# Reordering the work ahead of a mixture-of-experts loop: smaller one-hots, split gathers, a shorter index chain

## The chip, the cores and the metric

The kernel runs on one core of a Trainium2 chip. The engines of the core are TensorE (PE), VectorE (DVE), ScalarE (ACT), GpSimd (POOL) and SyncE (SP, here only an issuer of DMAs). The metric is the device time of one execution in microseconds, as the median of several runs.

## The reference

Four batches of 512 rows of width 256 go through two residual layers. Cut to what matters:

```python
# layer 1, per batch: x normed twice, through W_in, plus "depool" of the context
h = rmsnorm(layernorm(x), g_res) @ W_in + b_in
c = rmsnorm(ctx)[:, :256] * g_init
s[t] = a * s[t-1] + k * c[t]                       # a, k constants
plug = clip(cumsum(boundary_mask) - 1, 0, 1600)    # boundary_mask[cumsum(patch_lens) - 1] = 1
x = x + s[plug] + h
# layer 2: mixture of 8 experts, the best two of each row
p = softmax(layernorm(x) @ gate_w); w, e = top_k(p, 2); w = w / sum(w)
x = x + sum over the two of  w * (silu(z @ w1[e]) * (z @ w3[e])) @ w2[e]
```

The patch lengths (1601 per batch, integers) are an input, so the plug of a row is known only when their running sum has been taken: a mask has a one at each running sum less one that lies below 512, and the running sum of that mask says which row of the scan is added.

## The kernel before

Each engine has a program of its own, written out by hand in the order in which it issues; engines wait for one another on semaphores, and nothing else sets the order. The loop over about 37 blocks of 128 gathered rows (the experts' matmuls, all from the helper at L1545, and the elementwise work around them) begins at about 102 us and lasts to the end. It is not touched. What is touched is the work ahead of it, which goes through the four batches b = 0 to 3, each of TPB = 4 tiles of 128 rows.

The steps, by the names that they have in the code. **lengths** (VectorE): bytes of the lengths are scanned (L795), PE adds up the partitions (`prefix`, L1371), and a chain of short operations of 52 elements, each waiting for the one before, gives for each of the 13 x 4 columns the position below 512. **position(b)**: thirteen comparisons with 0..127 (L853) make a one-hot of the low seven bits, `onehot_lo`; `onehot_hi` is one of the two high bits (L843). **boundaries(b)** (PE, L1378): 13 matmuls of one against the other count the positions, 128 x 4 to a batch. **plugs** (VectorE L860, PE L1387 to L1391, VectorE L865, L868): mask, its running sum by a triangle of ones, `plugi` as indices for the gathers.

**stats_first(b)** (L875 to L886): mean and variance of x, and the sum of squares of the context that ScalarE's **squares(b)** (L616) made. **pow1(b)** (GpSimd, L490): the roots. **norm_first(b)**: on VectorE the scaled context `hp` (written L902, tile name hmul), on ScalarE the normed x (L625). **depool(b)** (PE, L1410, L1412): the scan as matmuls with a decay matrix. **depooled(b)** (VectorE, L910), **dep_out(b)** (SP): its rows to memory. **turned(b)** (PE, L1398): transposes of the normed x; **transposed_first(b)** (ScalarE, L634) copies them to memory. **through_win(b)** (PE, L1432): them through W_in, sixteen passes. **gather(b)** (GpSimd, L500): four indirect DMAs fetch rows of the depool by `plugi`. **second(b)** (VectorE, L919, L925, L928): x plus gathered rows plus through_win, and the statistics of the sum. **pow2(b)** (GpSimd, L506), **norm_second(b)** and **z(b)** (ScalarE, L643): the second norm. **router(b)** (PE, L1398 on z), copies (ScalarE, L651), **logits_of(b)** (PE, L1452), **route(b)** (VectorE): the choice of experts and each row's place in its expert's list.

At the end **lists** (PE, L1481) makes the list of row numbers per block, and VectorE turns it into indices: second_choice L1179, number L1182, unused L1185, idx_all L1188, gidx L1191, by which GpSimd gathers the rows of the first blocks (L529). blocks_i and five `stepm` operations (L1193 to L1203), steps (L1206) and some thirty more short ones make a table of control words, which all engines read before the loop (`table`, L1253). **keep_clock** (PE, L1488) is a matmul of zeros, 128 x 512, whose result nobody reads.

The buffers that tie the steps together: `ctx_sb` holds two contexts, so loads of contexts 2 and 3 wait for batches 0 and 1 (`next_ctx` on SP); `dg` holds gathered rows of two batches; `hp`, `nb1`, `vin` and the turned x have one or two.

## Time and profile before

| what | us |
|---|---|
| median of 3 runs | 444.62 (444.39 to 445.95) |
| the profiled execution | 445.63 |
| its span | 443.8 |
| PE busy in the span | 405.7 (91%) |
| VectorE busy | 303.2 (68%) |
| GpSimd busy | 243.2 (55%) |
| ScalarE busy | 193.7 (44%) |

The span is what the profiler saw of the core; the time of an execution has some 1.8 us around it. Busy shares are means over a loop and a prologue with different limits. In the rows below a line starts with its time in the span, then its duration, the engine, the source line and operation, what it writes and reads, and how many instructions it stands for; in brackets stands how long the engine idled before it and what ended that.

### The profile page before, as it was taken

To read this page: it belongs to the slowest core of one execution; us is meant where nothing else is said; L and a number is where in the kernel's file an instruction comes from. 1 tells how busy PE (TensorE), PEld (TensorE's weight loads), DVE (VectorE), ACT (ScalarE), POOL (GpSimd) and SP (SyncE) were. 2 spreads that over 40 slices of the span, in tenths; PEclk is the share of its full clock that TensorE was granted. 3 is DMA by queue.
4 is the path that set the end of the run, shared out by engine and by line. 5 is a ranking of instruction groups with operands and counts; after the bars stand their busy time and mean duration, and the time that the engine had idled before them with its cause. 6 is when DMAs were issued, how large, how long until landed. Compare 5 with 4: busy or idle time off the path is not lost.

```text
span 443.8 us, 12041 instructions
## 1 busy us (share of the span) xinstructions
PE 405.7 (91%) x2300; PEld 338.6 (76%) x2305; DVE 303.2 (68%) x826; ACT 193.7 (44%) x335; POOL 243.2 (55%) x251
## 2 busy tenths in 40 slices
PE   0669899969899999999999999999999999999983
PEld 0557686536678888888888888888888888788873
DVE  7995959887775577647775775577587546857450
ACT  2573527104543454335544553455445335634341
POOL 6328444313664676546665685576577445435443
PEclk9997969698999999999999999999999999999998
DMA  6953996702895788567887787789788655465652
GB/s 188 356 172 100 303 358 206 289 26 58 265 278 177 198 259 246 178 168 194 243 264 209 228 250 205 194 247 251 202 265 254 197 159 152 127 154 130 166 144 36
DMA packets 80362, 89.82 MB, mean 202 GB/s; under 512 B 8071, under 2 KB 60583, under 8 KB 80343
## 3 DMA queue, kind: packets, MB, share of 16 engines
q1 hardware_dynamic: 64327, 55.24, 38.4%
q0 software_dynamic: 16016, 34.37, 30.7%
q8 instruction: 6, 0.10, 0.1%
q14 instruction: 13, 0.11, 0.1%
HBM read 58.77 MB, written 30.82 MB: 202 GB/s over the span
## 4 chain that ended last, share of the span: by engine, by line
PE 70%; issue 3%; DVE 3%; ACT 1%; DMA 1%; DVEq 1%; POOL 0%; ACTq 0%; POOLq 0%
PE bank L1545 67%; PE bank L1552 2%; ACT split L341 1%; DMA out<-yblk,itok 1%; PE bank L1488 1%; DVE onehot_lo L1173 0%; POOL out L546 0%; ACT yblk L718 0%; DVE hT L1288 0%; DVE hmul L1272 0%; DVEq L295 0%; DVE swap_in L1280 0%; ACTq L341 0%; PE bank L1481 0%; DVE ctx_sb L951 0%
## 5 line engine op out<-in xcount | busy, mean ns | idle before, releaser
L1545 PE MATMUL bank<-split,xT_hi 128*128 x592 | 166.1, 402 | 4.4 <-issue 2.7
L1545 PEld LDWEIGHTS bank<-split,xT_hi 128*128 128x128 f32 x592 | 106.5, 189 | 27.9 <-issue 8.6
L1545 PEld LDWEIGHTS bank<-split,hT 128*128 128x128 f32 x888 | 111.5, 189 | 5.5 <-issue 1.5
L1545 PE MATMUL bank<-split,hT 128*128 (+1 forms) x888 | 113.3, 284 | 1.4 <-ACT yblk L718 0.7
L711 ACT ACTIVATE gact<-bank 128x512 f32<-128x512 f32 x74 | 44.3, 598 | 138.5 <-PE bank L1545 136.2
L1272 DVE TENSOR_TENSOR hmul<-gact,bank 128x512 f32<-128x512 f32 x74 | 50.8, 686 | 74.4 <-ACT gact L711 73.8
L1545 PE MATMUL bank<-split,xT_lo 128*128 x296 | 92.2, 393 | 0.0
L529 POOL DMA_INDIRECT xblk<-z_rows,gidx x40 | 41.0, 1024 | 89.6 <-DVE gidx L1295 69.8
L546 POOL DMA_INDIRECT out<-yblk,itok x37 | 71.0, 1919 | 32.1 <-issue 29.6
L347 DVE TENSOR_TENSOR split<-raw,split x22 | 50.3, 2292 | 25.9 <-ACT split L341 24.2
L1545 PEld LDWEIGHTS bank<-split,xT_lo 128*128 128x128 f32 x296 | 55.6, 188 | 12.3
L1280 DVE STREAM_TRANSPOSE swap_in<-hmul 128x512 f32<-128x512 f32 x74 | 52.6, 711 | 4.4
L1288 DVE TENSOR_TENSOR hT<-swap_out,hT 128x512 fp32r<-128x512 f32 x74 | 50.5, 683 | 4.8 <-ACT hT L706 3.8
L537 POOL DMA_INDIRECT wtok<-w_rows,widx x37 | 46.5, 1257 | 13.0 <-issue 11.0
L341 ACT ACTIVATE split<-raw (+1 forms) x24 | 45.8, 1915 | 7.5 <-issue 6.1
L280 POOL DMA_DIRECT2D raw<-in_L_ffn_w x56 | 38.0, 684 | 18.5 <-issue 18.5
L706 ACT ACTIVATE hT<-swap_out 128x512 fp32r<-128x512 f32 x74 | 46.5, 628 | 2.9 <-issue 2.0
L718 ACT ACTIVATE yblk<-bank,wtok 128x256 f32<-128x256 f32 x37 | 17.2, 464 | 34.9 <-PE bank L1545 32.3
L283 POOL DMA_DIRECT2D raw<-in_L_ffn_w x28 | 20.1, 724 | 5.3 <-issue 4.9
L1432 PE MATMUL bank<-win,batch 128*128 128x256 f32 x64 | 20.7, 495 | 0.8 <-DVE win L1101 0.5
L1488 PE MATMUL bank<-zeros,ones_b 128*128 128x512 bf16 x69 | 19.5, 435 | 1.5 <-issue 1.4
L1432 PEld LDWEIGHTS bank<-win,batch 128*128 128x128 f32 x64 | 16.0, 257 | 4.4 <-DVE x_all L925 0.7
(199 smaller groups left out, 336.0 us busy)
## 6 DMA issues: line engine op xcount, KB each, us to landing
raw<-in_L_ffn_w POOLq DMA_DIRECT2D x84, 256.0 KB
swap_rows<-swap_in SPq DMA_DIRECT2D x74, 256.0 KB, 3.7
swap_out<-swap_rows SPq DMA_DIRECT2D x74, 256.0 KB, 3.7
ctx_sb<-in_ctx SPq DMA_DIRECT2D x4, 1024.0 KB, 6.4
raw<-in_L_ffn_w SPq DMA_DIRECT2D x12, 256.0 KB, 6.6
x_all<-in_x SPq DMA_DIRECT2D x4, 512.0 KB, 8.4
depool_rows<-gact SPq DMA_DIRECT2D x4, 512.0 KB, 4.0
out<-x_all SPq DMA_DIRECT2D x4, 512.0 KB, 6.2
```

The costliest lines, as they stand in the source:

```text
L280: eng.dma_start(raw_up[:, ds(slot, 1), m, n >> 1, cols], rows).then_inc(signal, 16)
L341: act.activation(split_chunk[:, ds(raw3 * 2 + m, 1)], raw_chunk[:, ds(raw3 + m, 1)], ACT.Copy)\
L347: dve.tensor_tensor(split_chunk[:, ds(raw3 * 2 + m + 3, 1)], raw_chunk[:, ds(raw3 + m, 1)], split_chunk[:, ds(raw3 * 2 + m, 1)].bitcast(f3 ...
L529: pool.indirect_dma_start(xblk[:, q, :], None, z_dram[:, :], bass.IndirectOffsetOnAxis(ap=gidx[:, q:q + 1], axis=0))\
L537: pool.indirect_dma_start(wtok[:, q:q + 1], None, w_dram[:, :], bass.IndirectOffsetOnAxis(ap=widx[:, q:q + 1], axis=0))\
L546: pool.indirect_dma_start(out[:, :], bass.IndirectOffsetOnAxis(ap=itok[:, q:q + 1], axis=0), yblk[:, q, :], None, compute_op=ALU.add).then ...
L706: act.activation(hT_hi[:, q, ks].rearrange("p k (a t) -> p a k t", a=NQ), swap_out[:, q, part], ACT.Copy)\
L711: act.activation(gact[:, half * HALF:(half + 1) * HALF], p_gate[half][:, :], ACT.Silu)\
L1272: dve.tensor_tensor(hmul[:, cols], gact[:, cols], p_lin[part][:, :], ALU.mult)\
L1280: dve.transpose(swap_in[:, q, part].rearrange("p b k t -> p k b t"), hmul[:, part * HALF:(part + 1) * HALF].rearrange("p (k b t) -> p k b ...
L1288: dve.tensor_tensor(hT_lo[:, q, ks].rearrange("p k (a t) -> p a k t", a=NQ), swap_out[:, q, part], hT_hi[:, q, ks].bitcast(f32).rearrange( ...
L1545: mm = pe.matmul(out_, xp, w_, start=start and n == 0, stop=stop and n == 2)
```

## The change

- The positions are split as 32 by 16 in place of 128 by 4 (`LO`, `HI`). The one-hots of all batches are made by two comparisons over broadcast operands (`position_low`, `position_high`), and the 52 matmuls follow one another, 32 x 16 each. The mask is then 32 rows by (batch, tile, quarter), and the running sum takes 16 small matmuls with a triangle `upto_b`, which GpSimd makes and ScalarE copies.
- On VectorE the sums of x of batch 0 stand between the scan and the carries of the lengths (they wait for x of batch 0), its squares amid the last of the length operations; plugs and the mask move forward; the addition of through_win (`through_added`) moves from behind the gathered rows to ahead of them, and `second` adds the gathered rows last.
- Contexts 2 and 3 get memory of their own (the raw weights' second buffer, loaded later), all contexts and x are loaded in one sequence without waits; ScalarE squares two contexts in a row. The first raw load of that buffer waits for the last use of the contexts.
- Gathers are issued two tiles at a time, between the pow operations on GpSimd; two gathers of batches 2 and 3 each now stand ahead of pow2(0) and pow2(1).
- PE: 18 keep_clock matmuls behind the prefix and 5 behind the transposes of W_in; plugs ahead of depool(1); turned(1), turned(2), turned(3) each later by one depool or through_win; the first block's transposes ahead of the wait for the table. ScalarE's order of the copies and norms from norm_first(2) on is as before.
- Lists: rows of z are stored from row 1 on, row 0 is zeros, so the number in the list is the index. gidx comes straight from the list; unused and idx_all are made behind the table (`row_places`), and blocks_i and the stepm operations stand ahead of the wait for the lists. The GpSimd semaphore step ahead of the first two block gathers is left out.

The diff, cut to its core (renamed buffers, and bodies that only have other constants, are left out):

```diff
+            upto = zT[0:LO, 0:NA // 2, :].rearrange("p j d -> p (j d)").rearrange("p (a t) -> p a t", a=NA)
+            upto_b = zT[0:LO, NA // 2, :].bitcast(bf16).rearrange("p (a t) -> p a t", a=NA)
...
+            pos_lo = onehots[:, 0:B * CH * LO].rearrange("p (n c) -> p n c", c=LO)
+            pos_hi = onehots[:, B * CH * LO:B * CH * (LO + HI)].rearrange("p (n c) -> p n c", c=HI)
...
+        def ctx_of(b):
+
+            if b < 2:
+                return ctx_sb[:, b]
+            return raw[:, 1, (b - 2) * TPB * CD:(b - 1) * TPB * CD].rearrange("p (j d) -> p j d", d=CD)
...
-                sp.dma_start(ctx_sb[:, b % 2], ctx[b, 0:S, :].rearrange("(j p) d -> p j d", p=P))\
+                sp.dma_start(ctx_of(b), ctx[b, 0:S, :].rearrange("(j p) d -> p j d", p=P))\
...
-            load_x(1)
-            load_ctx(1)
-            load_x(2)
-            load_x(3)
+            for b in range(1, B):
+                load_ctx(b)
+                load_x(b)
...
-            next_ctx(2)
             dep_out(0)
-            next_ctx(3)
             dep_out(1)
...
+            pool.memset(upto, 1.0).then_inc(s["upto_ready"], 1)
+            pool.wait_ge(s["upto_ready"], 1)
+            pool.affine_select(out=upto, in_=upto, compare_op=ALU.is_ge, fill=0.0,
+                               base=0, pattern=[[-LO, NA], [1, P]], channel_multiplier=-1)\
+                .then_inc(s["upto_ready"], 1)
...
             pow1(1)
+            gather(0, (0, 1))
             pow1(2)
-            gather(0)
+            gather(0, (2, 3))
             pow1(3)
             gather(1)
+            gather(2, (0, 1))
             pow2(0)
-            gather(2)
+            gather(2, (2, 3))
+            gather(3, (0, 1))
             pow2(1)
-            gather(3)
+            gather(3, (2, 3))
             pow2(2)
             pow2(3)
...
             squares(0)
+            act.wait_ge(s["upto_ready"], 2)
+            act.activation(upto_b, upto, ACT.Copy).then_inc(s["upto_ready"], 1)
             norm_first(0)
             squares(1)
+            squares(2)
             transposed_first(0)
-            squares(2)
             norm_first(1)
+            squares(3)
             transposed_first(1)
-            squares(3)
             norm_first(2)
...
+            def position_low():
+
+                full3 = [P, NBC, LO]
                 dve.wait_ge(s["iota_ready"], 3)
-                dve.tensor_tensor(onehot_hi[:, :, :], iota_m8[:, :].unsqueeze(1).broadcast_to([P, NBC, TPB]),
-                                  hif.unsqueeze(2).broadcast_to([P, NBC, TPB]), ALU.is_equal)\
-                   .then_inc(s["onehot_ready"], 1)
-
-            def position(b):
-
-                if b >= 2:
-                    dve.wait_ge(s["count_ready"], b - 1)
-                for k in range(CH):
-                    n = b * CH + k
-                    ins = dve.tensor_scalar(onehot_lo[:, b % 2, k, :], iota_b[:, :], low[:, n:n + 1], None,
-                                            ALU.is_equal)
-                ins.then_inc(s["onehot_ready"], 1)
+                dve.tensor_tensor(pos_lo, iota_f[:, 0:LO].unsqueeze(1).broadcast_to(full3),
+                                  low.unsqueeze(2).broadcast_to(full3), ALU.is_equal).then_inc(s["onehot_ready"], 1)
+
+            def position_high():
+
+                full3 = [P, NBC, HI]
+                dve.wait_ge(s["carry_step"], lengths_done[0])
+                dve.tensor_tensor(pos_hi, iota_less[:, :].unsqueeze(1).broadcast_to(full3),
+                                  hif.unsqueeze(2).broadcast_to(full3), ALU.is_equal).then_inc(s["onehot_ready"], 1)
...
+            def through_added(b):
+
+                dve.wait_ge(s["hn_ready"], TPB * (b + 1))
+                xb = x_all[:, b * TPB:(b + 1) * TPB, :]
+                for n in range(PAIRS):
+                    dve.wait_ge(s["hmm_ready"], b * TPB + 2 * n + 2)
+                    dve.tensor_tensor(pair(xb, n), pair(xb, n), pH[n][:, :], ALU.add).then_inc(s["xh_ready"], 1)
...
-            lengths()
-            stats_first(0)
-            position(0)
+            lengths_scanned()
+            sums_first(0)
+            lengths_placed(lengths_carried(), lambda: squares_in(0))
             norm_first(0)
-            position(1)
+            position_low()
+            position_high()
+            depooled(0)
+            plugs()
             stats_first(1)
-            position(2)
-            depooled(0)
+            plugs_end()
+            scale_win()
             norm_first(1)
-            position(3)
             stats_first(2)
             depooled(1)
-            plugs()
-            scale_win()
-            plugs_end()
             norm_first(2)
             stats_first(3)
+            through_added(0)
             depooled(2)
             norm_first(3)
             second(0)
             depooled(3)
+            through_added(1)
             norm_second(0)
             second(1)
             norm_second(1)
             route(0)
+            through_added(2)
             second(2)
             places_beside_route(0)
             norm_second(2)
+            through_added(3)
...
-            dve.wait_ge(s["list_mm"], 1)
-            dve.tensor_copy(second_choice[:, :], p_idx)\
-               .then_inc(s["idx_step"], 1)
-            dve.wait_ge(s["idx_step"], 1)
-            dve.scalar_tensor_tensor(number[:, :], p_idx, -1.0, second_choice[:, :], ALU.mult, ALU.max)\
-               .then_inc(s["idx_step"], 1)
-            dve.wait_ge(s["idx_step"], 2)
-            dve.scalar_tensor_tensor(unused[:, :], number[:, :], 0.0, ids_f[:, B * TPB:B * TPB + 1]
-                                     .broadcast_to([P, TABLE]), ALU.is_equal, ALU.mult).then_inc(s["idx_step"], 1)
-            dve.wait_ge(s["idx_step"], 3)
-            dve.scalar_tensor_tensor(idx_all[:, :], number[:, :], -1.0, unused[:, :], ALU.add, ALU.add)\
-               .then_inc(s["idx_ready"], 1)
-            dve.wait_ge(s["idx_ready"], 1)
-            dve.tensor_copy(gidx[:, :], idx_all[:, 0:2]).then_inc(s["gidx_ready"], 2)
...
+            dve.wait_ge(s["list_mm"], 1)
+            dve.tensor_copy(second_choice[:, :], p_idx)\
+               .then_inc(s["idx_step"], 1)
...
+            dve.scalar_tensor_tensor(gidx[:, :], p_idx[:, 0:2], -1.0, second_choice[:, 0:2], ALU.mult, ALU.max)\
...
-            def boundaries(b):
-
-                pe.wait_ge(s["onehot_ready"], b + 2)
-                for k in range(CH):
-                    mm = pe.matmul(p_count[:, b * TPB:(b + 1) * TPB], onehot_lo[:, b % 2, k, :],
-                                   onehot_hi[:, b * CH + k, :], start=(k == 0), stop=(k == CH - 1))
+            def boundaries():
+
+                pe.wait_ge(s["onehot_ready"], 2)
+                for b in range(B):
+                    for k in range(CH):
+                        n = b * CH + k
+                        mm = pe.matmul(p_count[:, b * HI:(b + 1) * HI], pos_lo[:, n, :], pos_hi[:, n, :],
+                                       start=(k == 0), stop=(k == CH - 1))
                 mm.then_inc(s["count_ready"], 1)
...
+                for a in range(NA):
+                    pe.matmul(p_plug, upto_b[:, a, :], bmask[:, :, :, a].rearrange("p b j -> p (b j)"),
+                              start=(a == 0), stop=False)
...
             prefix()
+            pe.wait_ge(s["pad_ready"], 1)
+            pe.wait_ge(s["bf16_ready"], 2)
+            keep_clock(18)
 
             pe.wait_ge(s["small_in"], 16 * 5)
             for k in range(KD):
@@ -1495,24 +1545,22 @@
                     mm = pe.transpose(p_win[:, k * D + m * P:k * D + (m + 1) * P], win[:, m, k * P:(k + 1) * P],
                                       ident[:, :])
             mm.then_inc(s["wT_ready"], 1)
-            boundaries(0)
+            keep_clock(5)
             depool(0)
+            boundaries()
             turned(0)
-            boundaries(1)
-            boundaries(2)
+            plugs()
             depool(1)
-            boundaries(3)
-            turned(1)
-            plugs()
             through_win(0)
             depool(2)
-            turned(2)
+            turned(1)
             depool(3)
             through_win(1)
+            turned(2)
             router(0)
-            turned(3)
             logits_of(0)
             through_win(2)
+            turned(3)
             router(1)
...
+            xT(0, 0, 0)
             pe.wait_ge(s["table_ready"], 1)
             less_two = blocks_less_two(pe)
-            xT(0, 0, 0)
             keep_clock(4)
```

Three places in the order. First VectorE at the one-hots: in the kernel before (onehot_lo is written by position, hmul is the scaled context, gact the depooled rows, st and vin the statistics of x)

```order
L853 TENSOR_SCALAR onehot_lo<-iota_b,ln_v 128x128 x13
L894 SCALAR_TENSOR_TENSOR nb<-mv,rs 128x4
L902 SCALAR_TENSOR_TENSOR hmul<-ctx_sb,rs,ginit 128x256 x4
L853 TENSOR_SCALAR onehot_lo<-iota_b,ln_v 128x128 x13
L875 BN_STATS st<-x_all 128x6 x4
L878 BN_AGGR mv<-st 128x2 x4
L882 TENSOR_SCALAR vin<-sumsq 128x4
L886 TENSOR_SCALAR vin<-mv 128x4
L853 TENSOR_SCALAR onehot_lo<-iota_b,ln_v 128x128 x13
L910 TENSOR_TENSOR gact<-bank,bin 128x512 x2
```

and in the changed kernel, from the scaled context of batch 0 on:

```order
L936 SCALAR_TENSOR_TENSOR hmul<-ctx_sb,rs,ginit 128x256 x4
L873 TENSOR_TENSOR onehots<-iota_f,ln_v 128x1664
L880 TENSOR_TENSOR onehots<-iota_less,ln_v 128x832
L944 TENSOR_TENSOR gact<-bank,bin 128x512 x2
L886 TENSOR_SCALAR bmask<-bank 32x64
L901 BN_STATS st<-x_all 128x6 x4
L904 BN_AGGR mv<-st 128x2 x4
```

The four groups of thirteen comparisons, between which the steps of batches 0 and 1 stood, are two operations in a row, and the statistics of batch 1 now stand behind the mask, which waits for the counts.

Second PE around through_win(1) and (2) (win), with turned (bank from batch), router (from z) and logits (gate). Before:

```order
L1432 MATMUL bank<-win,batch 128x256 x8
L1398 MATMUL bank<-ident,z 128x128 x8
L1398 MATMUL bank<-ident,batch 128x128 x8
L1452 MATMUL bank<-gate,batch 128x8 x8
L1432 MATMUL bank<-win,batch 128x256 x8
L1398 MATMUL bank<-ident,z 128x128 x8
```

In the changed kernel:

```order
L1484 MATMUL bank<-win,batch 128x256 x8
L1450 MATMUL bank<-ident,batch 128x128 x8
L1450 MATMUL bank<-ident,z 128x128 x8
L1504 MATMUL bank<-gate,batch 128x8 x8
L1484 MATMUL bank<-win,batch 128x256 x8
L1450 MATMUL bank<-ident,batch 128x128 x8
L1450 MATMUL bank<-ident,z 128x128 x8
```

turned(3) stood between the first router and its logits; now turned(2) stands ahead of that router and turned(3) behind through_win(2).

Third VectorE behind the lists matmul (bank). Before:

```order
L1179 COPY second_choice<-bank 128x43
L1182 SCALAR_TENSOR_TENSOR number<-bank,second_choice 128x43
L1185 SCALAR_TENSOR_TENSOR unused<-number,ids_f 128x43
L1188 SCALAR_TENSOR_TENSOR idx_all<-number,unused 128x43
L1191 COPY gidx<-idx_all 128x2
L1193 TENSOR_SCALAR blocks_i<-cum 1x1
L1197 TENSOR_SCALAR stepm<-cum,ids_f 128x8
L1198 TENSOR_SCALAR stepm<-cum,ids_f 128x8
L1199 SCALAR_TENSOR_TENSOR stepm<-cum,ids_f,nblk 128x8
L1201 TENSOR_SCALAR stepm<-cum,ids_f 128x8
L1203 TENSOR_SCALAR stepm<-cum,ids_f 128x8
L1206 TENSOR_REDUCE steps<-stepm 128x5
```

In the changed kernel, where the wait for the lists is ahead of second_choice:

```order
L1218 TENSOR_SCALAR blocks_i<-cum 1x1
L1222 TENSOR_SCALAR stepm<-cum,ids_f 128x8
L1223 TENSOR_SCALAR stepm<-cum,ids_f 128x8
L1224 SCALAR_TENSOR_TENSOR stepm<-cum,ids_f,nblk 128x8
L1226 TENSOR_SCALAR stepm<-cum,ids_f 128x8
L1228 TENSOR_SCALAR stepm<-cum,ids_f 128x8
L1232 COPY second_choice<-bank 128x43
L1235 SCALAR_TENSOR_TENSOR gidx<-bank,second_choice 128x2
L1237 SCALAR_TENSOR_TENSOR number<-bank,second_choice 128x43
L1241 TENSOR_REDUCE steps<-stepm 128x5
```

The six operations that need no list now come ahead of it, and two of the five that need it are gone from here.

## Rows read from the trace of the kernel before

**Rows 1.** the page, chain of work that ended last, shares of the span by line

```profile
PE bank L1545 67%; PE bank L1552 2%; ACT split L341 1%; DMA out<-yblk,itok 1%; PE bank L1488 1%; DVE onehot_lo L1173 0%; POOL out L546 0%; ACT yblk L718 0%; DVE hT L1288 0%; DVE hmul L1272 0%; DVEq L295 0%; DVE swap_in L1280 0%; ACTq L341 0%; PE bank L1481 0%; DVE ctx_sb L951 0%
```

**Rows 2.** chain of waits of 90 to 104 us: start us, us, what

```profile
93.65 0.21 DVE number L1182
...
95.53 0.21 DVE stepm L1203
...
100.25 0.68 PE bank L1552 x2
100.94 1.71 PE bank L1488 x4
102.64 1.38 PE bank L1545 x4
```

**Rows 3.** groups by line, VectorE, 0-104 us: xcount, busy us, mean ns, idle before

```profile
L853 DVE TENSOR_SCALAR onehot_lo<-iota_b,ln_v 128x128 bf16<-128x128 bf16 x52 | 8.8, 241 | 0.0
...
L1173 DVE TENSOR_TENSOR onehot_lo<-iota_f,blk 128x688 f16<-128x688 f32 x2 | 1.7, 868 | 0.0
```

**Rows 4.** timeline of PE: start us, us, engine line op out<-in xcount [idle before]

```profile
12.75 1.11 PE L1495 MATMUL bank<-ident,win 128*128 128x128 f32 x4 [6.83 <-DMA gate<-in_L_ffn_gate_w]
...
16.20 2.04 PE L1410 MATMUL bank<-hmul,decayT 128*128 128x256 f32 x4
...
25.21 1.10 PE L1410 MATMUL bank<-hmul,decayT 128*128 128x256 f32 x4 [1.27 <-DVE hmul L902]
...
28.42 0.48 PE L1378 MATMUL bank<-onehot_hi,onehot_lo 128*128 128x4 bf16 x13
28.76 1.07 PE L1398 MATMUL bank<-ident,batch 128*128 128x128 f32 x8
...
32.41 6.75 PE L1432 MATMUL bank<-win,batch 128*128 128x256 f32 x16 [0.50 <-DVE win L1101]
39.00 1.03 PE L1410 MATMUL bank<-hmul,decayT 128*128 128x256 f32 x4
...
47.07 3.72 PE L1432 MATMUL bank<-win,batch 128*128 128x256 f32 x16 [0.29 <-DVE x_all L925]
...
56.71 6.54 PE L1432 MATMUL bank<-win,batch 128*128 128x256 f32 x16
...
64.52 1.92 PE L1452 MATMUL bank<-gate,batch 128*128 128x8 f32 x16 [0.22 <-ACT batch L651]
...
78.45 2.56 PE L1452 MATMUL bank<-gate,batch 128*128 128x8 f32 x16
```

**Rows 5.** windows, PE: stretch, us, busy us, granted clock, DMA share, GB/s

```profile
33.00:35.00 2.00, 2.00 (x6) 0.50 0.61 194
```

**Rows 6.** timeline of ScalarE

```profile
12.10 0.19 ACT L616 ACTIVATION_READ_ACCUMULATOR xblk<-ctx_sb 128x1 f32 x1
...
42.72 1.08 ACT L634 ACTIVATE batch<-bank 128x512 f32<-128x512 f32 x2 [6.72 <-PE bank L1398]
43.69 2.07 ACT L625 ACTIVATE batch<-x_all,nb,rs 128x256 f32<-128x256 f32 x4
50.31 2.08 ACT L643 ACTIVATE z<-x_all,nb,rs 128x256 f32<-128x256 f32 x4 [4.55 <-DVE nb L939]
...
68.97 2.08 ACT L643 ACTIVATE z<-x_all,nb,rs 128x256 f32<-128x256 f32 x4 [4.10 <-DVE nb L939]
```

**Rows 7.** timeline of GpSimd

```profile
30.37 1.64 POOL L490 TENSOR_TENSOR rs<-vin,neg_half 128x8 f32<-128x8 f32 x1 [7.33 <-DVE vin L886]
...
34.41 0.97 POOL L500 DMA_INDIRECT dg<-depool_rows,plugi  x1 [0.30 <-issue]
```

**Rows 8.** timeline of VectorE

```profile
24.59 1.66 DVE L902 SCALAR_TENSOR_TENSOR hmul<-ctx_sb,rs,ginit 128x256 f32<-128x256 f32 x4
...
28.29 1.39 DVE L875 BATCH_NORM_STATS2 st<-x_all 128x6 f32<-128x256 f32 x4
...
61.88 1.23 DVE L919 TENSOR_TENSOR x_all<-x_all,dg 128x1024 f32<-128x1024 f32 x1 [2.61 <-DMA dg<-depool_rows,plugi]
```

134 lines of the change are left out of this document (75 added, 59 removed).

## Prediction, made before the changed kernel had run

> **What bounds the kernel now.** First the page's shares of the chain: two thirds of the span are the expert matmuls of the loop [rows 1]. The diff leaves the loop's work alone, so the change is worth what it moves the loop's first matmul, which starts at 102.64 in the chain of waits [rows 2]. Then the stretch ahead of it, engine by engine. The lists are copied out in the two operations that end at 93.86 (the second is L1182) and the chain from there is VectorE [rows 2]. What the lists wait for is z of batch 2, which ScalarE begins at 68.97 after VectorE's routing of batch 1; that follows logits(1) on PE, 64.52 + 1.92 = 66.44, by 2.53 us [rows 4, 6]. From z(2) on the order is the same in both kernels, so the question is when logits(1) ends. Before that point no engine is full: PE waits 1.27 for VectorE ahead of depool(1), ScalarE 6.72 for PE, VectorE 2.61 for gathered rows [rows 4, 6, 8]. The third thing to see is PE's clock. through_win(0) and (2) take 6.75 and 6.54 us, through_win(1) 3.72 for the same sixteen passes, and the granted clock inside the first of them is 0.50, the lower of its two levels, 1.2 GHz against 2.4 [rows 4, 5].
>
> The profiled run took 445.63 us with a span of 443.8; the median of the three runs is 444.62. I sum differences of the profiled execution and take them off the median.
>
> **One-hots: much work saved, little time.** 52 comparisons, 8.8 us of VectorE, go [rows 3]. Two wide ones come, 1664 and 832 elements per partition. Nearest rows: 688 elements in 0.868 and 1024 in 1.23 [rows 3, 8], so 1.08 ns for each further element: 1.23 + 640 x 1.08 ns = 1.92, and 0.868 + 144 x 1.08 ns = 1.02, 2.94 together (3.15 if all went at 0.868/688; 2.6 at the slope alone). VectorE is spared some 6 us. But the order decides. squares(0) ends at 12.29 [rows 6]; with about 0.3 for two small operations, 1.64 of pow [rows 7] and 1.66 of scaling [rows 8], VectorE reaches the one-hots at 15.9 and ends them at 18.8. The 52 count matmuls, at 0.48 for 13 [rows 4], end at 20.7; the mask takes 0.2; then stats_first(1), which from its start to its pow took 30.37 - 28.29 = 2.08 [rows 7, 8], then pow 1.64: 24.6. With 0.15 and a first product of 0.45, depool(1) starts at 25.2. Before it started at 25.21 [rows 4]. The one-hots used to fill the time in which pow and the counts were awaited; now VectorE waits instead. This part: 0.
>
> **23 keep_clock matmuls.** They lie where PE idled 6.83 for the last small load [rows 4]. From 5.92 on, 18 of them take 7.7 at the half-clock rate of 1.71 for four [rows 2], then the transposes 1.1, then five more 2.2: 16.9 at the latest; depool(0) can have its first input at 14.9. Before, its first four matmuls took 2.04, against 1.10 for those of depool(1) [rows 4]. If the full clock comes in the 18, depool(0) needs 3.2 and is done before the counts can start at 18.8: cost 0. If it never comes, depool(0) needs about 5.9 and ends at 22.8: 4.0 late. I take 0, since a long dense run brought the clock back in through_win(0), whose next matmuls are fast again [rows 4]. The Trainium skill ("TensorE: Matmul & The Clock Gate", What's actually happening) says that the idle state is the throttled one and activity releases it; that agrees with the slow first matmuls, and by it too the cost here is 0.
>
> **PE from depool(1) on.** A depool at full clock is 28.42 - 25.21 = 3.2 [rows 4]. A through_win is 3.55 net: in through_win(0) the next matmul starts 0.16 before the row ends [rows 4]. After a turned, ScalarE starts 0.55 later (half of 1.07) and ends its copies 0.97 after that; norm_first takes 2.07, z 2.08 [rows 4, 6].
> plugs is now ahead of depool(1), so through_win(0) follows directly: 25.2 + 3.2 + 3.55 = 31.95 (before 39.0, with a half-clock pass). depool(2) to 35.15. turned(1) comes behind it, and its copies and norm_first(2) end at 35.15 + 0.55 + 0.97 + 2.07 = 38.75. Scaling of batch 3 (0.6 to the first product) and depool(3): 42.55. through_win(1): 46.1, before 50.8. Here turned(2) now stands, and ScalarE still has its copies and norm_first(3) ahead of z(0): 46.1 + 3.59 = 49.7, z(0) to 51.8, before 52.4 (50.31 + 2.08) [rows 6]. PE's lead of 4.7 us shrinks to 0.6: this is the new wait that the order brings. A copy of 0.55 and logits(0), 1.92: 54.3. through_win(2) to 57.8, before 63.25. turned(3), 0.55 and 0.97, and z(1), 2.08: 61.4. The copy and logits(1): 63.9, before 66.44. Gain at z(2): 2.5 us, if no pass falls to half clock.
>
> **Gathers and own context memory.** Each gather costs GpSimd 0.97 + 0.30 [rows 7]. Two of batch 2 now stand ahead of pow of z(0): 2.5 us later there. z(0) cannot start before 49.7 for ScalarE's sake, which covers it; without that cover it costs up to 2.5. The early gathers remove VectorE's wait of 2.61 [rows 8], but logits(1) is next late, so no gain beyond the 2.5 above. Contexts 2 and 3 in the raw buffer drop a wait on SP; at most 0.
>
> **Lists to loop.** From 93.86 to 95.74 VectorE runs unused, idx_all, gidx, blocks_i and five stepm operations [rows 2]: 1.88. The first two leave the chain, the last six move into the wait for the lists, which is about 0.6 long for 0.9 of work (0.3 stays), and a narrow gidx (0.2) stays: gain 1.4. PE's transposes of block 0, 0.68 [rows 2], move ahead of the table; VectorE's xT_lo is next late about half a microsecond earlier than 102.64: gain 0.5 (0 to 0.7).
> Behind z(2) logits(3) took 2.56 against 1.92 [rows 4], a half-clock stretch too; without it another 0.6.
>
> **Sum at full clock:** 2.5 + 1.4 + 0.5 + 0.6 = 5.0, so 439.6.
>
> **The clock, and the rivals.** In the sum PE idles or runs only transposes and narrow matmuls in three places ahead of dense passes: 20.7 to 25.2, 35.2 to 39.4, and 46.1 to 54.3. Before, such stretches ended differently: the one that ends at 25.21 left depool(1) at full rate, those of 28.42 to 32.41 and 50.8 to 56.71 were followed by half-clock passes [rows 4, 5]. A fall costs 6.75 - 3.72 = 3.0 or 6.54 - 3.72 = 2.8, less what it loses in slack: 2.3 to 3.0, taken as 2.7. The third stretch, longer than either that brought the fall before, is the likeliest place.
>
> *Forecast, one fall:* 5.0 - 2.7 = 2.3 gained, 442.3. Chance 0.33.
> *No fall (rival 1):* 439.6; for it speak the 23 extra matmuls and plugs in the first stretch. 0.27, and 0.05 for still more, about 437, should the early loads and gathers pull VectorE forward where I found it waiting.
> *Two falls (rival 2):* 5.0 - 5.4 = 0.4 slower, 445.0. The gain of the index chain is given back. 0.17.
> *Three falls (rival 3, the other side):* 5.0 - 8.1 = 3.1 slower, 447.7. It decides when all of through_win(0), (1) and (2) read 6.5 us or more, against two of three before. The Trainium skill's table ("Why this matters for your kernels", same page) speaks against idle gaps between matmul bursts in the middle of a kernel, and by it all three gaps would count; the trace bears that out in two of three cases. 0.10.
> *The warm-up does not do what it says (rival 4):* depool(0) at half rate, 4.0 of delay against 5.0 of gain, 443.6, or 446.3 with a fall. 0.08.
>
> **How the numbers follow.** The predicted time is the forecast's, 442.3. The range must leave out 2 in 10: from 438.0, below rival 1, to 447.5, where rival 3 begins. Half a per cent, 2.2 us, is about what a measurement of this kernel can tell from no change. Faster by more than that: no fall and better, 0.32, and about half of the forecast's case, 0.16: 0.48. Within: the rest of it, most of rival 2 and some of rival 4: 0.34. Slower: 0.18.
>
> **What would show it.** After the change: onehots in two rows of 1.9 and 1.0; VectorE idle for the counts and the pow around 20 to 25; depool(1) at about 25; the three through_win rows near 3.7, one perhaps 6 or more; ScalarE idle for PE ahead of the copies of turned(1), (2) and (3); z(2) near 66 to 69; VectorE's two operations between list and steps. The forecast is wrong if depool(1) starts well before 25 (then the one-hots do pay), if z(0) waits for GpSimd, or if the loop itself, with its first raw loads and gathers moved, changes its length of 341 us.

## The result, and the profile after

The changed kernel takes 456.12 us (median of 4 executions, 452.55 to 457.01); the kernel before, on the same chip, 444.5 (4 executions, 442.07 to 445.95). The ratio is 1.025, with a 95% interval of 1.018 to 1.032: slower by 11.6 us, outside the forecast range of 438.0 to 447.5.

The profiled execution took 457.01 (span 455.4) against 445.63 (span 443.8). Its 11.6 us of span split at three marks:

| stretch | before | after | difference |
|---|---|---|---|
| start to the end of the lists matmul (L1481, now L1533) | 93.37 | 103.13 | +9.76 |
| lists to the loop's first matmul | 8.96 | 7.11 | -1.85 |
| from there to the loop's first silu (gact on ScalarE) | 3.56 | 3.11 | -0.45 |
| first silu to the end | 337.91 | 342.05 | +4.14 |

The gain of the index chain is there, but not made up as forecast. VectorE's rows behind the lists, before and after:

```profile
99.15 0.19 DVE L1253 CAST table<-bank 1x43 int32<-1x43 f32 x1 [0.33 <-PE bank L1537]
99.46 2.29 DVE L1312 TENSOR_TENSOR split<-raw,split 128x2048 fp32r<-128x2048 f32 x1
101.67 0.42 DVE L1265 TENSOR_TENSOR xT_lo<-bank,xT_hi 128x256 fp32r<-128x256 f32 x1
```

```profile
107.07 0.19 DVE L1288 CAST table<-bank 1x43 int32<-1x43 f32 x1 [0.33 <-issue]
107.37 2.29 DVE L1355 TENSOR_TENSOR split<-raw,split 128x2048 fp32r<-128x2048 f32 x1
109.58 0.42 DVE L1308 TENSOR_TENSOR xT_lo<-bank,xT_hi 128x256 fp32r<-128x256 f32 x1
```

The table starts 5.78 behind the lists before and 3.94 after, so 1.84 is won by then. From the table to xT_lo it takes 2.52 before and 2.51 after, since VectorE is busy with split: PE's earlier transposes of the first block bring nothing. The 0.45 ahead of the first silu is the clock: on the loop's first matmuls PE's windows of one microsecond show a granted clock of 0.50 at 102 to 103 and 0.79 at 103 to 104 in the kernel before, and 1.00 at 110 to 114 after; the first four take 1.69 and 1.20.

Two losses outweigh the gain, one in the prologue and one in the loop, of which the diff changes one copy and the operations in front of it.

For the prologue, first PE by stretches of ten microseconds (stretch, its length in us, busy us and instructions, granted clock, DMA share, GB/s):

```profile
20.00:30.00 10.00, 6.83 (x47) 0.68 0.61 214
30.00:40.00 10.00, 8.22 (x41) 0.98 0.36 119
40.00:50.00 10.00, 8.30 (x26) 0.66 0.92 279
50.00:60.00 10.00, 6.67 (x35) 0.71 0.88 285
60.00:70.00 10.00, 8.52 (x36) 0.78 0.51 160
70.00:80.00 10.00, 9.95 (x50) 0.66 0.41 139
```

A stretch of ten with a granted clock of c had 20 x (1 - c) us at the lower level, 1.2 GHz. Added up, that is 30.7 us of the sixty (from the same windows at one microsecond each); the kernel before has 14.1, nearly all in the two slow passes of [rows 4]. The timeline of PE tells where (start us, us, engine line operation, what it writes and reads, count, idle before and what ended it):

```profile
18.80 1.47 PE L1428 MATMUL bank<-onehots 128*32 128x16 bf16 x52 [0.57 <-DVE onehots L880]
...
24.95 2.04 PE L1462 MATMUL bank<-hmul,decayT 128*128 128x256 f32 x4 [3.17 <-DVE hmul L936]
...
30.71 3.62 PE L1484 MATMUL bank<-win,batch 128*128 128x256 f32 x16
...
41.70 2.04 PE L1462 MATMUL bank<-hmul,decayT 128*128 128x256 f32 x4 [3.48 <-DVE hmul L936]
...
55.44 2.07 PE L1450 MATMUL bank<-ident,z 128*128 128x128 f32 x8 [3.33 <-issue]
57.31 3.58 PE L1504 MATMUL bank<-gate,batch 128*128 128x8 f32 x16
60.74 5.54 PE L1484 MATMUL bank<-win,batch 128*128 128x256 f32 x16
66.12 1.04 PE L1450 MATMUL bank<-ident,batch 128*128 128x128 f32 x8
68.53 1.81 PE L1450 MATMUL bank<-ident,z 128*128 128x128 f32 x8 [1.38 <-ACT z L659]
...
70.57 2.89 PE L1504 MATMUL bank<-gate,batch 128*128 128x8 f32 x16
73.31 6.08 PE L1484 MATMUL bank<-win,batch 128*128 128x256 f32 x16
...
87.84 3.06 PE L1504 MATMUL bank<-gate,batch 128*128 128x8 f32 x16
```

Five pieces of dense work run at the lower level: depool(1) at 24.95 (four matmuls in 2.04, against 1.10 in [rows 4]), depool(3) at 41.70, logits(0) with through_win(2), the end of logits(1) with through_win(3), and logits(3). Ahead of the first three PE idled 3.2 to 3.5 us, ahead of the others it had transposes and narrow matmuls with short waits. The first follows a wait for VectorE's scaled context, which ahead of the same depool(1) took 1.27 in [rows 4] and left the clock up.

The lateness reaches ScalarE through the copies of the turned x, which in its order stand ahead of the next norm (timeline of ScalarE; L650 are these copies, L659 is z):

```profile
51.77 1.08 ACT L650 ACTIVATE batch<-bank 128x512 f32<-128x512 f32 x2 [10.91 <-PE bank L1450]
...
66.81 1.08 ACT L650 ACTIVATE batch<-bank 128x512 f32<-128x512 f32 x2 [8.67 <-PE bank L1450]
...
75.98 2.07 ACT L659 ACTIVATE z<-x_all,nb,rs 128x256 f32<-128x256 f32 x4 [5.00 <-DVE nb L976]
```

z(1), behind the second of these rows, starts at 67.79, and z(2) at 75.98, against 68.97 in [rows 6].

The loop's loss shows in the page's groups (count, busy us, mean ns) and at its start on VectorE:

```profile
L1593 PE MATMUL bank<-split,xT_hi 128*128 x592 | 167.8, 405 | 4.8 <-issue 2.3
...
L1593 PE MATMUL bank<-split,xT_lo 128*128 x296 | 93.0, 395 | 0.0
```

```profile
112.17 0.20 DVE L1293 SCALAR_TENSOR_TENSOR unused<-number,ids_f 128x43 f32<-128x43 f32 x1
...
113.12 0.20 DVE L1303 TENSOR_TENSOR widx_all<-unused,second_choice 128x43 int32<-128x43 f32 x1
115.38 0.69 DVE L1315 TENSOR_TENSOR hmul<-gact,bank 128x512 f32<-128x512 f32 x1 [2.06 <-issue]
```

The first silu had ended at 113.95, and hmul follows 1.43 later: the five row_places operations, and what VectorE's sequencer issues behind them without a busy row, come in between. In the kernel before three such operations stand there, and they end at 104.77, 1.72 ahead of the end of the silu.

### The profile page after: what moved, and what is told of

Its sections match the earlier page's. It is cut to its first block and busy times, and to the rows that moved or that the text cites. A ratio compares the mean times of both kernels' runs of the same rounds, so it can differ in the third digit from the quotient of the medians.

```text
span 455.4 us, 12058 instructions
## 1 busy us (share of the span) xinstructions
PE 417.6 (92%) x2334; PEld 344.1 (76%) x2339; DVE 297.9 (65%) x775; ACT 194.1 (43%) x336; POOL 243.9 (54%) x253
## 5 line engine op out<-in xcount | busy, mean ns | idle before, releaser
L1593 PE MATMUL bank<-split,xT_hi 128*128 x592 | 167.8, 405 | 4.8 <-issue 2.3
L1414 PE MATMUL bank<-zeros,ones_b 128*128 128x512 bf16 x92 | 25.5, 431 | 1.7 <-issue 1.6
L508 POOL DMA_INDIRECT dg<-depool_rows,plugi x16 | 16.1, 1005 | 12.9 <-DMA depool_rows<-gact 7.9
L1414 PEld LDWEIGHTS bank<-zeros,ones_b 128*128 128x128 bf16 x96 | 10.2, 113 | 13.9 <-issue 6.8
```

Source lines behind the costliest of these rows:

```text
L1593: mm = pe.matmul(out_, xp, w_, start=start and n == 0, stop=stop and n == 2)
```

## The experiments

The theory after the first comparison: the prologue is late because PE idles in new places and its clock falls; what the order itself changes is small. Its rivals: the later places of turned alone, whatever the clock; the split gathers, which delay GpSimd's pow. For the loop: row_places at its start, and, as the loop's matmuls are longer throughout, the place of its buffers in memory. The table gives every run: median us, ratio to the kernel before on the same chip with its 95% interval (median of the kernel before 442.9 to 443.3, beside the changed kernel 444.5), and of the profiled execution the us at the lower clock between 20 and 80, the start of z(2), the end of the lists, and the loop from the start of the first silu to the end. The runs come from several chips, so medians are compared by their ratios.

| kernel | median | ratio | lower clock | z(2) | lists | loop |
|---|---|---|---|---|---|---|
| before, as shown above | 444.62 | | 14.1 | 68.97 | 93.37 | 337.91 |
| changed | 456.12 | 1.025 (1.018 to 1.032) | 30.7 | 75.98 | 103.13 | 342.05 |
| e_keepgaps | 445.9 | 1.0065 (1.0036 to 1.0093) | 0 | 67.83 | 92.06 | 342.34 |
| e_turned | 446.28 | 1.0068 (1.004 to 1.0095) | 17.1 | 68.92 | 92.95 | 341.44 |
| e_both | 445.57 | 1.0059 (1.0034 to 1.0083) | 13.7 | 69.19 | 93.21 | 339.96 |
| e_gather | 454.59 | 1.028 (1.018 to 1.038) | 20.5 | 72.78 | 99.17 | 341.11 |
| e_nokeep | 449.53 | 1.015 (1.010 to 1.020) | 1.8 | 68.14 | 92.90 | 342.40 |
| e_rows | 445.66 | 1.0044 (1.0016 to 1.0072) | 0 | 67.86 | 92.07 | 340.59 |
| b_same | 442.39 | one execution | 7.9 | 65.13 | 90.17 | 338.31 |
| b_keep | 443.55 | 1.0012 (0.9992 to 1.0033) | 6.8 | 66.48 | 90.70 | 338.17 |
| b_shift | 444.95 | 1.0062 (1.004 to 1.0084) | 13.5 | 65.91 | 90.15 | 339.34 |
| a_pad | 451.83 | 1.023 (1.019 to 1.027) | 20.5 | 73.06 | 99.48 | 340.06 |
| e_best | 440.65 | 0.9945 (0.9919 to 0.997) | 9.9 | 64.86 | 89.07 | 339.81 |
| e_pad | 439.85 | 0.9942 (0.9908 to 0.9976) | 3.4 | 65.12 | 89.13 | 337.89 |

**e_keepgaps: the gaps filled, the order kept.** keep_clock gets a bank nobody uses there.

```diff
             plugs()
+            keep_clock(12, 6)
             depool(1)
...
             turned(1)
+            keep_clock(15, 6)
             depool(3)
...
             turned(2)
+            keep_clock(14, 6)
             router(0)
...
             turned(3)
+            keep_clock(7, 6)
             router(1)
```

> The changed kernel with its order, plus keep_clock matmuls into a spare bank where PE idled: 12 ahead of depool(1), 15 ahead of depool(3), 14 ahead of router(0), 7 ahead of router(1). Rival A (the clock alone): every through_win and depool(1), depool(3) at full rate (3.6 and 3.2 us), the lists end near 90 and the time is 440 to 444. Theory 1 with the order as a cause of its own: full rate, but ScalarE still waits for each turned, the lists end at 92 to 97 and the time is 445 to 450. Rivals B and C: little change, above 452.

Measured: 445.9, 0.65% above the kernel before in place of 2.5%. PE's timeline and one of its windows:

```profile
21.77 2.76 PE L1414 MATMUL bank<-zeros,ones_b 128*128 128x512 bf16 x12
25.01 1.10 PE L1462 MATMUL bank<-hmul,decayT 128*128 128x256 f32 x4 [0.48 <-DVE hmul L936]
28.10 3.62 PE L1484 MATMUL bank<-win,batch 128*128 128x256 f32 x16
...
53.58 1.95 PE L1504 MATMUL bank<-gate,batch 128*128 128x8 f32 x16
55.39 3.70 PE L1484 MATMUL bank<-win,batch 128*128 128x256 f32 x16
...
50.00:60.00 10.00, 9.54 (x56) 1.00 1.01 340
```

depool(1) starts when it did (25.01 against 24.95), so nothing but its rate has changed; through_win(0) follows 2.61 sooner, and the lists end at 92.06, 11.07 sooner. That the clock costs the prologue its loss against this profile of before is shown: only multiplied zeros were added. With no lower clock at all, z(2) starts at 67.83; the prediction's sum had it at 66.5.

The missing 1.3 comes in at depool(2), with the split gathers. Timelines of GpSimd, VectorE and PE (L508 is a gather, L498 pow1):

```profile
28.33 1.09 POOL L508 DMA_INDIRECT dg<-depool_rows,plugi  x1 [4.07 <-DMA depool_rows<-gact]
...
30.72 1.69 POOL L498 TENSOR_TENSOR rs<-vin,neg_half 128x8 f32<-128x8 f32 x1
...
32.44 0.16 DVE L928 SCALAR_TENSOR_TENSOR nb<-mv,rs 128x4 f32<-128x4 f32 x1 [3.26 <-POOL rs L498]
...
33.18 1.10 PE L1462 MATMUL bank<-hmul,decayT 128*128 128x256 f32 x4 [1.46 <-issue]
```

The first two gathers of batch 0 stand ahead of pow1(2) and wait for the depooled rows in memory. pow1(2) starts 2.6 later than in e_gather below, VectorE waits for it, and PE waits 1.46 ahead of depool(2). In the changed kernel the slow depool(1) hides this: its depool(2) has no wait.

**e_turned: turned(1), (2), (3) at their old places**, all else as changed.

```diff
             depool(1)
+            turned(1)
             through_win(0)
             depool(2)
-            turned(1)
+            turned(2)
             depool(3)
             through_win(1)
-            turned(2)
             router(0)
+            turned(3)
             logits_of(0)
             through_win(2)
-            turned(3)
```

> The changed kernel with PE's turned(1), turned(2), turned(3) back at the places they had before (ahead of through_win(0), ahead of depool(3), behind router(0)); all else as changed. Theory 1 (the later turned make ScalarE wait for PE and PE for ScalarE, and the waits drop PE's clock): ScalarE's waits of 8.9 and 10.9 us for turned(1) and (2) shrink, the lists end near 90 to 92 instead of 103.1, at most three half-clock passes, time 439 to 444. Rival A (the gaps' clock alone, wherever turned stands): the gap of 3.2 us ahead of depool(1) stays, so depool(1) stays at 6 us, and the time stays above 450. Rival B (split gathers ahead of pow2) and rival C (VectorE waits for counts and pow behind the two wide one-hots): no change, 453 to 457.

Measured: 446.28, between the 439 to 444 of the theory and the 450 of rival A. Nearly as much is won as by the zeros, though depool(1), logits(0) and through_win(2) still run at the lower level:

```profile
40.00:50.00 10.00, 7.78 (x37) 1.00 0.98 313
50.00:60.00 10.00, 9.31 (x35) 0.55 1.06 389
```

```profile
39.66 1.10 PE L1462 MATMUL bank<-hmul,decayT 128*128 128x256 f32 x4 [0.47 <-DVE hmul L936]
...
56.03 6.27 PE L1484 MATMUL bank<-win,batch 128*128 128x256 f32 x16
```

The wait of 3.48 ahead of depool(3) is 0.47 again, its fall is gone, and so are those of through_win(3) and logits(3). The gap ahead of depool(1) and the fall at logits(0) stay. The later places of turned thus bring three of the five falls, and a chain on which each fall is paid.

**e_both: both together, with zeros in the first gap alone** (the order of e_turned, and keep_clock(12, 6) ahead of depool(1)).

> turned(1) to (3) at their old places and 12 keep_clock matmuls in the gap ahead of depool(1). Theory 1: the lists end at 88 to 91, time 437 to 442, the fastest of these. Rival A: as the kernel with the four filled gaps. Rivals B and C: above 450.

Measured: 445.57, no better than either, where the theory had 437 to 442. depool(1) is fast and through_win(0) starts at 29.0, but the clock now falls from 48 to 61, over router(0), logits(0) and through_win(2), and the lists end at 93.21. What the first zeros win is mostly gone before that: through_win(0) starts 2.67 earlier than in e_turned, depool(3) only 0.34 (39.32 against 39.66), since depool(2) again waits for GpSimd and depool(3) for VectorE. The longer fall takes the rest.

**e_gather: the gathers undivided at their old places.**

```diff
             pow1(1)
-            gather(0, (0, 1))
             pow1(2)
-            gather(0, (2, 3))
+            gather(0)
             pow1(3)
             gather(1)
-            gather(2, (0, 1))
             pow2(0)
-            gather(2, (2, 3))
-            gather(3, (0, 1))
+            gather(2)
             pow2(1)
-            gather(3, (2, 3))
+            gather(3)
```

> The changed kernel with the gathers of a batch undivided and at their old places between the pow operations. Theory 1 and rival A: the same as the changed kernel, 453 to 457, since z(0) waits for ScalarE's copies and not for pow2. Rival B (the divided gathers hold up pow2): z(0) and z(1) 2.5 us earlier, time 450 to 453 or less.

Measured: 454.59 (451.78 to 457.65), with a ratio inside the interval of the changed kernel. In this order, with its falls, the split gathers are neither the loss nor a gain: against a_pad below, whose falls are the same, z(2) starts at 72.78 in place of 73.06. pow1(2) does come earlier, as said above (GpSimd):

```profile
28.09 1.64 POOL L498 TENSOR_TENSOR rs<-vin,neg_half 128x8 f32<-128x8 f32 x1 [3.80 <-DVE vin L912]
```

What undivided gathers are worth with the gaps filled was not tested; the 1.46 of e_keepgaps says that it need not be nothing.

**e_nokeep: e_keepgaps without the 18 and the 5 early zeros.**

```diff
-            keep_clock(18)
...
-            keep_clock(5)
             depool(0)
```

> The kernel with the four filled gaps, without the 18 and 5 keep_clock matmuls ahead of depool(0). By the sum of the prediction: depool(0) at half rate, 5.9 us, ending near 21 to 23 instead of 18, the counts and depool(1) later by 0 to 4 us; with the gaps still filled, the time rises by as much, 446 to 450. Rival: depool(0) is off the path, time as with the 23, 445 to 446.5.

Measured: 449.53, a ratio of 1.015 against 1.0065 for e_keepgaps, some 3 us. In the profiled execution depool(0) takes 2.04 for four matmuls, as depool(1) does at a granted clock of 0.50 in the changed kernel (the windows here say 1.00 at 15 to 20, so the level is read from the duration); depool(1) starts at 26.92 in place of 25.01, and the lists end 0.84 later; the profile, of the fastest of four executions, shows less than the medians. The early zeros do what the prediction took them to do: with them depool(0) takes 1.10.

**e_rows: e_keepgaps with row_places moved** from ahead of the loop's first hmul to behind it (into the first step, ahead of weight_index).

```diff
-            row_places()
-            dve.wait_ge(s["idx_step"], 6)
...
                 next_index(i + 3, 1 - q, half + q + 1)
+                if not after(i, 1):
+                    row_places()
+                    dve.wait_ge(s["idx_step"], 6)
                 weight_index(i, q, half)
```

> The kernel with the four filled gaps, and row_places (five operations on VectorE, 1.15 us) moved from ahead of the loop into the first step, behind next_index. Theory 2 (row_places delays the first hmul by 1.5 us, and with it the next block, so the index chain's gain is given back): VectorE's first hmul follows its gact within 0.7 us as before, PE's wait of 1.36 us for xT_lo of the next block shrinks below 0.5, time 1.0 to 1.5 us less than the kernel with filled gaps (445.9), so 444.4 to 444.9. Rival D (the register loads behind it, 2 us of issue, set the first hmul): no change, 445.5 to 446.5.

On VectorE the first hmul now follows the silu, which ends at 102.91, at once:

```profile
102.94 0.69 DVE L1315 TENSOR_TENSOR hmul<-gact,bank 128x512 f32<-128x512 f32 x1 [1.74 <-ACT gact L730]
...
105.44 0.20 DVE L1303 TENSOR_TENSOR widx_all<-unused,second_choice 128x43 int32<-128x43 f32 x1
```

From the first silu to the third it takes 6.00 (e_keepgaps 7.44, before 5.97). That 1.4 repeats: the seven profiles with row_places ahead of the loop have 7.41 to 7.44, e_rows, e_best and e_pad 6.00 to 6.05, the kernel before 5.97 to 6.34 in four. The whole loop is 1.75 shorter here, but six profiles with the same loop and places (changed, e_keepgaps, e_turned, e_both, e_gather, e_nokeep) spread from 339.96 to 342.40, so that figure is known no better than to 2.4. The medians, 445.66 and 445.9, don't separate the two, and the time lies where rival D had it, though the hmul above, which waits for nothing but the silu, speaks against D; the gain rests on the profiles.

**b_shift: the kernel before, with its loop's small buffers moved.** In the changed kernel the new one-hots and mask take other sizes, so n_i to itok, a few short tensors, and behind them xblk, xT_hi, xT_lo and yblk lie 288 bytes lower in their partitions. Here they lie 224 bytes higher than before.

```diff
+        sb("spacer", [P, 56], f32)
         n_i = sb("n_i", [P, E], i32)
```

> The kernel before with 224 bytes of unused memory ahead of the small tensors behind swap_out, so that xblk, xT_hi, xT_lo and yblk start 224 bytes later; nothing else differs. In the changed kernel xT_hi starts at byte 221984 of its partition, before at 222272; here it starts at 222496, which lies as the changed kernel's does in its block of 256 bytes. If the place of these buffers is what lengthens the loop, the loop's matmuls from xT_hi rise from a mean of 401 ns to 404 or 405, the loop from its first silu gets 1.5 to 2.5 us longer than the 338 of before (339.5 to 340.5), and the time is 1.5 to 2.5 us above the kernel before on this chip. If the place does not matter: 401 ns, 338, and within 0.5 us of the kernel before.

The two groups of the unchanged kernel (b_same), and of b_shift:

```profile
L1545 PE MATMUL bank<-split,xT_hi 128*128 x592 | 165.7, 402 | 4.4 <-issue 3.1
...
L1545 PE MATMUL bank<-split,xT_lo 128*128 x296 | 92.3, 393 | 0.0
```

```profile
L1546 PE MATMUL bank<-split,xT_hi 128*128 x592 | 168.7, 406 | 3.3 <-issue 1.7
...
L1546 PE MATMUL bank<-split,xT_lo 128*128 x296 | 93.0, 395 | 0.0
```

3.0 + 0.7 us more busy PE, and a kernel 0.6% slower (interval 1.004 to 1.0084), for a buffer that nobody reads. In the profile the loop is 1.0 to 1.4 longer than in the three profiles of the kernel before with its buffers in place, less than expected; PE idles 1.1 less ahead of the xT_hi matmuls.

**a_pad: the changed kernel with 288 bytes of spacer**, so that these buffers lie as before (`[P, 72]` in the same line).

> The changed kernel with the same 288 bytes and nothing else. If the place of the buffers lengthens the loop: 454.0 to 454.6 where the changed kernel took 456.1, loop from its first silu 340 in place of 342.05; the lists still end at about 103 and half clock still fills five stretches. If it does not matter: 456.1 and 342.

The xT_hi group is back at 402 ns, 2.0 us less busy PE, and xT_lo at 393, 0.7 less:

```profile
L1594 PE MATMUL bank<-split,xT_hi 128*128 x592 | 165.8, 402 | 5.0 <-issue 2.4
```

The loop takes 340.06, 2.0 shorter than in the changed kernel's profile but inside the spread of those six. The ratios, 1.023 and 1.025, have intervals that overlap, so the time doesn't show the gain. In this profile depool(3) is not slow (20.5 us at the lower clock against 30.7, as in e_gather): how many falls an execution has varies. That the place costs time is shown by b_shift; how much of the changed kernel's time it is, rests on the duration of the matmuls.

**b_keep: the kernel before with zeros in its own gaps**, to price its two slow passes.

```diff
+            pe.wait_ge(s["pad_ready"], 1)
+            pe.wait_ge(s["bf16_ready"], 2)
+            keep_clock(7, 6)
             plugs()
...
+            keep_clock(2, 6)
             router(0)
+            keep_clock(4, 6)
             turned(3)
```

> The kernel before with matmuls of zeros in its own gaps (7 ahead of plugs, 2 ahead of router(0), 4 ahead of turned(3)) and nothing else. If the clock is what the gaps cost, through_win(0) and (2) fall from 6.75 and 6.54 to 3.7, through_win(0) ends 3 us sooner, and the time is 1.5 to 4 us below the kernel before, since some of its runs show only one slow pass. If another engine is next late (gathers, GpSimd's pow), the passes read 3.7 but the lists do not end sooner than 90.2, as in the undisturbed look at the kernel before, and the time is within 1 us of it.

All four through_win take 3.7, and the time stays: 443.55, ratio 1.0012. Two falls come elsewhere, in depool(1) from 26.3 and in logits(2) from 70.7. PE, then VectorE:

```profile
32.82 3.70 PE L1432 MATMUL bank<-win,batch 128*128 128x256 f32 x16
...
54.24 3.72 PE L1432 MATMUL bank<-win,batch 128*128 128x256 f32 x16 [0.31 <-DVE x_all L925]
```

```profile
51.63 1.23 DVE L919 TENSOR_TENSOR x_all<-x_all,dg 128x1024 f32<-128x1024 f32 x1 [3.78 <-DMA dg<-depool_rows,plugi]
```

VectorE waits 3.78 for gathered rows, which a faster through_win does not bring sooner. **b_same** is the kernel before once more:

> The kernel before, unchanged, for a trace of it on the chip of these runs (its runs there had a median of 442.9). If the traced order is the whole story, the lists end at 91 to 94 and the stretch from the first loop matmul to the end is 341 to 342 us, as in the trace before. If that stretch is the same in the changed kernel's order too (345 there), the loop lost nothing.

Its through_win(0) and (2) are fast without any zeros, and it takes 442.39 (PE and ScalarE):

```profile
32.37 3.72 PE L1432 MATMUL bank<-win,batch 128*128 128x256 f32 x16 [0.50 <-DVE win L1101]
...
47.24 2.08 ACT L643 ACTIVATE z<-x_all,nb,rs 128x256 f32<-128x256 f32 x4 [4.56 <-DVE nb L939]
```

In b_shift, whose order is the same, through_win(2) is slow again:

```profile
53.47 6.73 PE L1433 MATMUL bank<-win,batch 128*128 128x256 f32 x16
```

and yet its lists end at 90.15, as in b_same at 90.17 (which has a fall of its own from 61.8, in through_win(3)) and in b_keep, where both passes are fast, at 90.70. In the order before, then, a slow through_win(2) cost nothing in these profiles. A slow through_win(0) seems to: the profile of before alone has one [rows 4], its z(0) starts at 50.31 [rows 6] against 47.24 to 47.89 in the other three, and its lists end 2.7 to 3.2 later. That is one profile against three, not an experiment. In how many executions that happens the times don't tell.

**e_best and e_pad: what was learnt, together.** e_best has turned at its old places, zeros in the gaps (12 ahead of depool(1), 7 ahead of depool(3), 10 ahead of router(0), 3 ahead of turned(3)) and row_places moved; e_pad is e_best with the 288 bytes.

> turned(1) to (3) at their old places, keep_clock matmuls in the gaps that this order leaves (12 ahead of depool(1), 7 ahead of depool(3), 10 ahead of router(0), 3 ahead of turned(3)), and row_places in the first step. Theory 1 with theory 2: no half-clock pass, lists end at 86 to 89, first loop matmul near 94 to 96, time 438 to 441, faster than the kernel before. Rival E (the loop's first weights or another transfer are next late): lists early, but the time stays at 443 or above.

> The version with turned at its old places, zeros multiplied in the gaps and the row places moved into the loop, with 288 bytes of unused memory, so that xblk to yblk lie where the kernel before has them. If the place lengthens the loop: matmuls from xT_hi at 401 ns in place of 404, the loop from its first silu at about 338 in place of 339.8, time 438.5 to 439.3 where the version without the spacer took 440.65. If the place does not matter: 404 ns and 440.65 again.

Measured: 440.65 and 439.85, both 0.6% faster than the kernel before (0.9945 and 0.9942, intervals below 1). Their profiles are not free of falls: 9.9 and 3.4 us at the lower clock, with a through_win(3) of 5.06 and 5.39, behind no gap. e_best against e_rows, both at full clock up to 59.9 us and with other places of turned, tells the price of the order alone: z(2) at 64.86 against 67.86, 3.0. In e_pad the loop takes 337.89, that of the kernel before; the 0.8 between the medians is within their spread.

## Why the prediction was wrong

**What held.** The one-hots are two operations of 1.88 and 1.02 (forecast 1.92 and 1.02; its bound "at the slope alone" should have read 2.7, and nothing rests on it) and bring nothing, because VectorE then waits for counts and pow (0.36 and 0.70): depool(1) starts at 24.95, forecast 25.2. The 23 zeros warm PE for depool(0); rival 4 did not happen, and e_nokeep shows what it would have been. Lists to loop: 1.85 gained, forecast 1.4 + 0.5, but that the sum fits is luck: VectorE's part brought 1.84, since all six operations fit into the wait for the lists, and the earlier transposes 0.0, since xT_lo stands behind VectorE's split. The three gaps in which PE would idle (20.7 to 25.2, 35.2 to 39.4, 46.1 to 54.3) were named where they came: 22 to 25, 38 to 41.7, 52 to 55.4.

**The step that failed first: how many falls.** I took one, at the third gap, because of three such gaps in [rows 4, 5] only two had brought a fall; the case of all three had a chance of 0.10. All three gaps brought one, and two more followed, at through_win(3) and logits(3), where I had counted 0.6 as won. (At full clock that term is worth 0.2: from z(2) to the lists 24.23 in e_keepgaps, before 24.40.) The Trainium skill's table that stood beside rival 3 ("TensorE: Matmul & The Clock Gate", Why this matters for your kernels), by which all three gaps would count, is borne out here: idle 3.17, 3.48 and 3.33 ahead of 24.95, 41.70 and 55.44, and the lower level behind each.

The price of a fall, 2.7, was not too low. Against e_keepgaps the lateness grows by 2.6 in depool(1), by 1.1 up to the end of depool(3) (0.9 is left of the first at its start), 1.6 in router(0) and logits(0), 1.8 in through_win(2), 1.0 in logits(1), 1.9 behind through_win(3), 0.5 up to logits(3) and 0.5 from there to the lists: 11.07 for five, 2.2 each.

**The second: the kernel that it was measured against.** The 2.5 won at z(2) came from a profile of before whose slow through_win(0) had made it 3 us late, and I counted the end of that fall as a gain of the new order. In b_same, b_shift and b_keep z(2) starts at 65.1 to 66.5; against those the changed order, even at full clock (e_keepgaps, 67.83), loses 1.4 to 2.7 where I had it win 2.5. It is already there at z(0), 50.98 against 47.24, 3.7 later. The sum had z(0) at 49.7, so 2.5 of it is the later copies of turned, which I had seen shrink PE's lead to 0.6. The other 1.3 is a wait that the sum did not have: I looked at the gathers ahead of pow2 alone and called them covered, but those ahead of pow1(2) hold up depool(2) by 1.46, and in this order turned(1) and norm_first(2) pass that on. With turned at its old places and the same gathers z(0) starts at 47.23 (e_best).

**The third: the loop.** I held its 341 us fixed and gave its length as one thing that would make the forecast wrong. It is 4.14 longer from the first silu. row_places takes 1.4 of it (first to third silu), which I let "leave the chain" without saying which instruction stands behind it: the loop's first hmul. The place of the buffers, which I did not look at, takes 2.5 more busy PE than before (167.8 + 93.0 against 166.1 + 92.2), gone in a_pad and e_pad. With both put right, in e_pad, the loop is back at 337.89. The split of the 4.14 is no finer than this, since the loop of one and the same code varies by up to 2.4.

Put together: -1.85 from the index chain and -0.45 ahead of the first silu, +9.76 by clock and order, +4.14 in the loop, 11.6.

## What to carry to other kernels

Before pricing a pass at the lower clock, ask what ends last beside it, and whether the profile you measure against has one of its own: a slow through_win(2) was free in one order and paid for in the other, where ScalarE's next norm stood behind transposes that PE made only after its dense work. When an order opens gaps on PE, fill them with matmuls of zeros in an unused bank in every gap, not in the first alone (lists at 93.21 in e_both, 89.07 in e_best), and expect that some falls stay. And after any change in the sizes of early buffers, compare the mean duration of the untouched loop's matmuls: a spacer can bring it back.

## What the hardware showed that was not expected

Moving the loop's small buffers by 288 or 224 bytes made the matmuls from xT_hi take 404 to 406 ns in place of 402 to 403, and those from xT_lo 395 in place of 393, at an unchanged place of the weights in split; those from hT, which did not move, stayed at 283 to 284. xT_hi starts at byte 222272 of its partition in the fast kernels, a multiple of 64, and at 221984 or 222496 in the slow ones, multiples of 32 alone. Which of the moved buffers does it, and by what mechanism, was not separated; weight loads from xT_hi take 188 to 189 ns either way.

Transposes, narrow matmuls and short waits alone were enough for a fall: in the changed kernel no idle time of PE between through_win(2) and through_win(3) was longer than 1.38, and the latter still took 6.08. Nor did one and the same wait always end alike: behind the 1.27 ahead of depool(1) the clock stayed up in the profile of before and in b_same, and fell in b_shift and b_keep, whose programs on PE are the same up to there.
